# A decoder layer in split fp32: turned key buffers, a later latent, query splits moved into the first attention step, weight splits by GpSimd

## What is computed

```
x = x + memory_attention(layernorm(x))     # 8 heads used, sig = elu(q)+1, (sig @ M) / (sig @ z + eps), @ Wo.T
x = x + cross_attention(layernorm(x), ctx) # 16 sequences of 64 queries, 64 context and 64 latent keys,
                                           # 4 key heads x 8 query heads of 128, softmax, @ Wo
x = x + experts(layernorm(x))              # router: softmax over 64, top 8; out = flat * w_sum + w_dense @ expert_bias
```

## Time and profile before

| | |
|---|---|
| median of three runs | 720.72 us (719.70 to 722.87) |
| the profiled execution | 720.87 us |
| its span, first to last instruction | 719.1 us |
| mean granted clock of TensorE, of full speed | 0.993 |
| busy: PE, its weight loads, DVE, ACT, POOL | 96%, 81%, 71%, 49%, 16% |
| the chain that ended last, by engine | PE 83%, DVE 8%, DMA 2%, ACT 2%, POOL 1% |
| moved | 90.1 MB, 125 GB/s over the span |

### The profile page before, as it was taken

The page is one execution under the profiler, slowest core; times in us unless marked ns, Lnnn a source line. Parts: engine busy times, 40 slices in busy tenths (PEclk is TensorE's granted clock), DMA queues, the critical chain, the costliest instruction groups (busy, mean ns, idle before and its releaser), DMA issues.

```text
span 719.1 us, 10998 instructions
## 1 busy us (share of the span) xinstructions
PE 692.9 (96%) x3562; PEld 581.1 (81%) x3562; DVE 510.3 (71%) x1078; ACT 349.5 (49%) x1042; POOL 115.8 (16%) x121
## 2 busy tenths in 40 slices
PE   8999699999999998999999999999999999899995
PEld 6888588887887787888888888888888888688874
DVE  2764877678725878677677876767977566778876
ACT  4454655456244446344445643554645336555541
POOL 0175400000101332020120220210202000022410
PEclk9999999999999999999999999999999999999998
DMA  9888510001234456543242833423542404221101
GB/s 329 296 288 286 205 59 1 1 0 59 88 118 143 135 170 206 189 147 100 77 126 80 263 102 102 146 87 110 194 146 78 146 31 154 75 82 59 59 16 58
DMA packets 69997, 90.14 MB, mean 125 GB/s; under 512 B 4224, under 2 KB 47232, under 8 KB 69952
## 3 DMA queue, kind: packets, MB, share of 16 engines
q1 hardware_dynamic: 64160, 80.13, 34.2%
q10 hardware_dynamic: 5792, 9.44, 3.7%
HBM read 62.29 MB, written 27.26 MB: 125 GB/s over the span
## 4 chain that ended last, share of the span: by engine, by line
PE 83%; DVE 8%; DMA 2%; issue 2%; ACT 2%; POOL 1%; SPq 0%; POOLq 0%; ACTq 0%; DVEq 0%
PE bank L896 23%; PE bank L828 19%; PE bank L652 14%; PE bank L965 7%; PE bank L1014 5%; PE bank L798 5%; PE bank L991 4%; PE bank L643 1%; DMA raw<-in_L_attn_Wo 1%; PE bank L765 1%; DVE regA L1364 1%; PE bank L687 1%; PE bank L731 1%; DVE forms L1364 1%; DMA raw<-in_ctx 1%
## 5 line engine op out<-in xcount | busy, mean ns | idle before, releaser
L896 PE MATMUL bank<-regA,oT 128*128 128x512 f32 x768 | 180.6, 391 | 3.1 <-DVE oT L1364 3.1
L896 PEld LDWEIGHTS bank<-regA,oT 128*128 128x128 f32 x768 | 143.4, 188 | 33.3 <-DVE oT L1364 3.9
L1290 ACT ACTIVATE probs<-bank,negmax 128x128 f32<-128x128 f32 x256 | 90.1, 378 | 46.0 <-DVE negmax L1741 46.0
L828 PE MATMUL bank<-xnT,forms 128*128 128x512 f32 x384 | 97.2, 397 | 0.2
L828 PEld LDWEIGHTS bank<-xnT,forms 128*128 128x128 f32 x384 | 70.1, 188 | 15.2 <-DVE qbuf L1571 1.7
L828 PE MATMUL bank<-regC,forms 128*128 128x512 f32 x288 | 75.8, 401 | 2.4 <-DVE qbuf L1571 2.4
L1044 ACT CAST oT<-bank 128x512 fp32r<-128x512 f32 x64 | 37.6, 588 | 79.3 <-PE bank L1014 76.5
L1044 ACT CAST pT<-bank 128x512 fp32r<-128x512 f32 x64 | 34.7, 592 | 69.5 <-PE bank L991 69.5
L652 PE MATMUL bank<-regC,xnT 128*128 128x512 f32 x256 | 67.8, 396 | 0.0
L965 PEld LDWEIGHTS bank<-k_ring,qbuf 128*128 128x128 f32 x512 | 62.0, 191 | 2.5
L828 PEld LDWEIGHTS bank<-regC,forms 128*128 128x128 f32 x288 | 52.8, 190 | 12.9 <-DVE qbuf L1571 2.4
(11 more groups left out here) (151 smaller groups left out, 1072.0 us busy)
## 6 DMA issues: line engine op xcount, KB each, us to landing
q_dram<-qbuf SPq DMA_DIRECT2D x32, 512.0 KB, 3.0
qbuf<-q_dram SPq DMA_DIRECT2D x31, 512.0 KB, 4.5
raw<-in_L_attn_Wo SPq DMA_DIRECT2D x8, 1024.0 KB, 7.6
raw<-in_L_xattn_Wo SPq DMA_DIRECT2D x4, 2048.0 KB, 9.9
wq_raw<-in_L_xattn_Wq SPq DMA_DIRECT2D x16, 512.0 KB, 4.1
k_ring<-keys_dram SPq DMA_DIRECT2D x32, 128.0 KB, 3.6
v_raw<-vals_dram SPq DMA_DIRECT2D x64, 64.0 KB, 3.5
rawk<-in_L_xattn_Wv SPq DMA_DIRECT2D x4, 512.0 KB, 4.0
```

The lines of the kernel that those rows point to most:

```text
L828: last = nc.tensor.matmul(k_bank[:, :], forms[:, p[1], a, i, c, :], right(b)[:, c, :], start=j == 0, stop=j == 5)
L896: last = nc.tensor.matmul(bank[7][:, :], oT[:, a, h, :], wo[:, b, h, :], start=h == 0 and i == 0, stop=h == GH - 1 and i == 2)
L1290: last = nc.scalar.activation(probs[:, bb, p, :], bank[bb][:, p * P:(p + 1) * P], ACT.Exp, bias=negmax[:, bb, p:p + 1], accum_out=rowsum[: ...
```

## The change

- The three buffers of `save_kv` are used in the order `kvout`, `qb`, `qneg`. ACT waits ahead of its loop for buffer 2, DVE for buffer 1, and for buffer 0 only ahead of its first denominators.
- The sixth latent's transposes, cast and split move from loop turn 17 to turn 18 on PE, ACT and DVE.
- The second split of the key weights leaves turn 18: ACT's casts go behind the third value copy, DVE's splits behind the eighth latent.
- The three summed casts and splits of pair 5 leave the last turn of the lead loop for the first attention step, on ACT behind the value cast, on DVE behind the value split. SP's program is as before.
- In step 0 of every group but the first ACT's last four weight casts go ahead of its context casts (`oT`). In group 3 DVE splits heads 0 and 1 ahead of its context splits, 2 and 3 behind them, and POOL splits 4 to 7.
- In step 7 of group 2 and step 1 of group 3 the last two heads of the projection go behind the probability transposes (in step 1 of group 3 so behind the router transposes too).

```diff
-        kv_slots = (qneg[:, :], qb[:, :], kvout[:, :])
+        kv_slots = (kvout[:, :], qb[:, :], qneg[:, :])
...
             def scale_expert(e):
...
+            for h in range(4, GH):
+                pool.wait_ge(wo_hi, GH * (KV - 1) + h + 1)
+                pool.wait_ge(wo_lo, GH * (KV - 1) + h)
+                nc.gpsimd.tensor_tensor(wo[:, 1, h, :], wo_raw[:, h, :], wo[:, 0, h, :].bitcast(F), ALU.subtract)\
+                    .then_inc(wo_lo, 1)
...
-                if output_in(i):
+                if output_in(i) and i != 2 * NT + 1:
                     latent_transposes(output_in(i) - 1)
+                if i == 2 * NT + 2:
+                    latent_transposes(output_in(i - 1) - 1)
...
-            def project(g, t, release):
+            def project(g, t, release, heads=range(GH)):
...
-                pe.wait_ge(oT_lo, 2 * n + 2)
-                pe.wait_ge(proj_added, n + 1)
-                for h in range(GH):
+                if heads[0] == 0:
+                    pe.wait_ge(oT_lo, 2 * n + 2)
+                    pe.wait_ge(proj_added, n + 1)
+                for h in heads:
...
+                divided = not pair and not (last_group and t >= 2) and t
+                front = range(GH - 2) if divided else range(GH)
                 if not first_step:
                     if t == 0:
                         project(g - 1, 7, True)
                     else:
-                        project(g, t - 1, False)
+                        project(g, t - 1, False, front)
...
                 elif pair:
                     product_5(pair)
                     product_3(pair)
+                elif divided:
+                    project(g, t - 1, False, range(GH - 2, GH))
...
-            act.wait_ge(kv_written[0], kv_count(0, 16))
+            act.wait_ge(kv_written[2], kv_count(2, 16))
...
-                if i == 2 * NT + 2:
-                    wkv_high(1, wkv2, 2, 0)
-                if output_in(i):
-                    latent_high(output_in(i) - 1)
+                    latent_high(output_in(i - 1) - 1)
...
+                if t == 2:
+                    wkv_high(1, wkv2, 2, 0)
...
                 copy_1(p)
-                summed_high(p + 1, (p + 1) % 2)
+                if p < LEAD:
+                    summed_high(p + 1, (p + 1) % 2)
...
-                if t % 2 and has_pair(g, t + 2):
+                if first_step or t % 2 and has_pair(g, t + 2):
                     summed_high(pair + 1, slot)
...
+                if t == 0 and not first_step:
+                    act.wait_ge(proj_done, 8 * g)
+                    for h in range(4, GH):
+                        wo_high(g, h)
                 for bb in range(2):
...
-                if t == 0 and not first_step:
-                    act.wait_ge(proj_done, 8 * g)
-                    for h in range(4, GH):
-                        wo_high(g, h)
...
+                    if s == 0:
+                        dve.wait_ge(kv_written[0], kv_count(0, 16))
...
-            for r in (1, 2):
-                dve.wait_ge(kv_written[r], kv_count(r, 16))
+            dve.wait_ge(kv_written[1], kv_count(1, 16))
...
-                if i == 2 * NT + 2:
-                    wkv_low(1, wkv2, 3 * KC, 0)
...
             x_low(tr("latent", NT - 1), NT - 1)
+            wkv_low(1, wkv2, 3 * KC, 0)
...
-                summed_low(p + 1, (p + 1) % 2)
                 if p < LEAD:
+                    summed_low(p + 1, (p + 1) % 2)
...
-                if t % 2 and has_pair(g, t + 2):
+                if first_step or t % 2 and has_pair(g, t + 2):
                     summed_low(p + 1, slot)
...
-                    for h in range(2 if p is not None else 0, 4):
+                    for h in range(2) if p is None else range(2, 4):
                         wo_low(g, h)
...
-                    for h in range(4, GH):
+                    for h in range(2, 4) if p is None else range(4, GH):
                         wo_low(g, h)
```

More of the change, by code:

```diff
@@ L1211, in _ @@
                     wkv_high(0, wkv2, 2, 1, (2 * (i % 2), 2 * (i % 2) + 1))
+                if output_in(i) and i != 2 * NT + 1:
+                    latent_high(output_in(i) - 1)
                 if i == 2 * NT + 2:
-                    wkv_high(1, wkv2, 2, 0)
-                if output_in(i):
-                    latent_high(output_in(i) - 1)
+                    latent_high(output_in(i - 1) - 1)
             def save_latent_values(t):
@@ L1529, in _ @@
                     wkv_low(0, wkv2, 2 * KC, 1, (2 * (i % 2), 2 * (i % 2) + 1))
+                if output_in(i) and i != 2 * NT + 1:
+                    x_low(tr("latent", output_in(i) - 1), output_in(i) - 1)
                 if i == 2 * NT + 2:
-                    wkv_low(1, wkv2, 3 * KC, 0)
-                if output_in(i):
-                    x_low(tr("latent", output_in(i) - 1), output_in(i) - 1)
+                    x_low(tr("latent", output_in(i - 1) - 1), output_in(i - 1) - 1)
                 if output_in(i) is not None and i != 2 * NT - 1:
```

## The result

| | before | after |
|---|---|---|
| median | 720.39 us (6 runs, 719.70 to 724.12) | 733.02 us (6 runs, 729.97 to 734.99) |
| the profiled execution | 720.87 | 734.94 |
| its span | 719.1 | 733.1 |
| mean granted clock of TensorE | 0.993 | 0.982 |

The ratio of the times is 1.016, with a 95% interval from 1.0124 to 1.0195. The ratios in this document are not exactly quotients of two medians (that would be 1.0175 here); where two edits are compared, the ratios decide, because every group of runs was set against its own runs of the kernel before. The change makes the kernel slower, by 12.6 us of the medians, 11.5 by the ratio. The forecast was 731.4 us in a range from 723 to 736.

A forecast was written before the change was run, and what follows sets the result against it. The prediction took TensorE, busy 96% of the span, as the bound. Its terms, 0 - 0.6 + 2.6 + 1.3 - 1.0 + 4.85 + 3.4 = +10.55, added to 720.87 gave 731.4 us, range 723 to 736.

The forecast's parts named there:

- Part 1: Memory stage, key buffers turned: `sig` could start earlier, gain given back at POOL's folds; 0, ends -5.6 and +1.7 us.
- the race of 72.30 against 72.33: Memory stage: `sig` would start at 72.30, POOL's fold at 72.33; just ahead or just behind, gain taken as 0.
- Part 2: Latent values, sixth latent's transposes later: PE then waits for the seventh, with one DVE split less ahead; -0.6 us.
- Part 3: Latent values, second key weight split later: block sums +5.05 us, PE pauses before the second latent key product; +2.6 us.
- Part 4: First attention step, splits behind first maxima: the second step's query load comes late, PE pauses 4.65 us; net +1.3 us.
- Part 5: Late output weights: -1.0 us in step 7 of group 2, +4.85 us from step 0 of group 3.
- (a): Step 7 of group 2: two heads, 1.37 us of PE, fill the pause of 1.01 before 602.82; -1.0 us.
- (b): Group 3, from step 0: POOL's four splits delay SP's router load, PE pauses 5.9 us before router transposes; +4.85 us.
- The clock: TensorE's granted clock falls once behind each of the pauses of 4.65 and 5.9 us; together +3.4 us.
- the clock stays up: Rival: TensorE's clock stays at its upper level behind both long pauses; 728.0 us, chance 0.18.
- The port went DVE's way: Rival, memory stage: DVE gets the shared port ahead of POOL and both PE pauses vanish; 725.8 us, chance 0.10.
- the loads are in time: Rival: second step's query slice and the router rows land before PE needs them; 717.2 us, chance 0.12.

The follow-up runs named there:

- a1: The changed kernel with the second key weight split put into slots where ACT and DVE idle; 727.13 us, ratio 1.009.
- a2: The changed kernel with SP loading pair 6 behind the first attention step's key, query and value loads instead of ahead; 726.93 us, ratio 1.0079.
- b5: The kernel before with the key buffers turned and POOL's last fold held until the second `sig` is done; 719.41 us, ratio 0.9985.
- b1: The kernel before with the key buffers turned and nothing else; 721.30 us, ratio 1.0013.
- a5: The changed kernel with 40 throwaway identity transposes on PE at the end of its first attention step; 730.93 us, ratio 1.0136.
- b6: The kernel before, key buffers as they were, with POOL's last fold held until the second `sig` is done; 718.73 us, ratio 0.9992.

## Why the prediction held, and where it was off

*Part 1, at 0.* The number was right, by luck in part. Of the two ways that the prediction gave for the race of 72.30 against 72.33, the kernel after shows one, `sig` ahead by 0.06: the denominators go through one by one between POOL's operations and the second pause grows. The kernel with the buffers alone shows the other. But the second pause did not grow by what the first lost: the first lost 2.2 us and the second grew by 0.4. What made 0 of the remaining 1.8 us is a fall of the clock behind the second pause, at 3.22, which stood only in the upper end of the part. The other traces agree. With the buffers turned and the folds free, the two pauses together are 2.2 to 4.4 us in nine traces (5.6 and 4.6 in the two with the buffers as before), but the granted clock fell behind the last of them in seven of the nine (0.62 to 0.65 over 4.5 us) and in neither of the two. That the buffers bring the fall is not shown by so few. The Trainium skill (SBUF — State Buffer, Who interferes with whom) states that a DVE instruction with two SBUF inputs contends with a GpSimd instruction that reads SBUF, and that the order of issue decides who blocks. The trace agrees: the 0.28 product that met an operation of POOL took 1.38, and `sig` 2.40 against 0.69 when it was first.

*Part 2, at -0.6.* PE's waits for the sixth and seventh latent were 1.13 and 0.41 us and are nothing and 1.13, so -0.4. The -0.5 of the table has part 1 in it, and a start of the stage 0.3 later (DVE's first biased query at 70.53 for 70.26).

*Part 3, at +2.6.* The pause was 2.62, through the five engines' steps as they were named. Its fall of the clock (0.66, 1.5 to 1.6 us) was left at the end of the range.

*Part 4, at +1.3.* The pause was 4.62 for 4.65, the landing 5.7; +1.6 at the second scores.

*Part 5.* (a) -1.3 for -1.0. (b) The pause was 5.33 for 5.9, POOL's four operations 6.08 for 6.4 (from 618.45 to 624.9). Two took 1.30 and two 1.55, beside DVE's probabilities, with 0.13 between: the disturbance was about 0.25 each and not 0.5. The 0.5 was said to come from the overlaps in rows 3, but those show DVE held by POOL and not the reverse. From issue to PE's transposes it was 4.9 for 5.1. +4.6 for 4.85.

*The clock* is where the sum was off. Two falls at 1.7 were counted, 3.4 us; the traced execution has four, and they took 1.7, 1.6, 2.7 and 2.6, together 8.6. The price was read from a window of 0.62 behind a short pause, a mixture of the levels. Behind the two long pauses PE got 0.50 throughout. That is 5.2 us more than in the sum, less 1.8 for part 1's shorter pauses; with small errors of both signs elsewhere the traced span grew by 14.0 where 10.55 were forecast. The median, 733.0, lies 1.6 above 731.4. The queues and their prices were right, but that the total came so near has luck in it: the traced execution is 3.5 us above the forecast, and 1.8 us of error in part 1's pauses hid as much of the clock's.

*The rivals.* That the clock stays up did not come true behind the long pauses: 0.50 behind both here, and 0.50 again in the runs that kept one of them (behind 4.06 in the run with the router later, behind 5.35 and 5.42 in the runs of a1 and a2). The port went DVE's way in the kernel after at the first `sig`, and the waits did not vanish. That the loads are in time was priced at -3.3 for the first step and 717.2 us in all. It didn't come true, but as a price it was good: the run with the loads moved gained 3.0 in that step, and 717.2 less the 2.6 of part 3, which that price still held, is 714.6, where the version in which all three are in time took 713.94.

Not tried: how the fall of the clock could be avoided behind the memory stage's pause, and whether a longer chain of POOL's splits could run before ACT's casts.

## What to carry to other kernels

Moving work off the path an engine waits on is paid at the next queue. Before a step is put later, list what every engine and the transfer queue hold in program order behind its last signal: two of the three losses here were loads that stood behind a split which had become later. One load was moved ahead, the consumer of the other was moved by a step, and the splits of the third loss went into idle slots; that turned 1.6% slower into 0.8% faster. Price a new pause with the low clock that may follow it: here another 1.5 to 2.7 us where it came.

## What the runs showed of the hardware

- Between 1.9 and 2.9 us the length of a pause did not decide whether the clock falls. Granted clock over 4.5 us behind PE's pauses in these traces: 0.62 behind 1.97 (before, first attention step), 0.66 behind 1.88 (b5), 0.65 behind 2.26 (the mended version), 0.62 behind 2.68 (b1), 0.66 behind 2.62 (after, latent values), 0.50 behind the same 2.62 in the run with the filler (a5); but 1.00 behind 2.77 and 2.86, behind 1.99 (b6), behind 2.48 (mended, buffers as before), behind 2.78 (a2), and behind the very pause of 2.62 before the latent key product in the run with the router later, whose program is the same up to there. Behind each of the eight pauses of 4.06 us and more it fell: to 0.50, but for a1's 4.46 with 0.66. What else decides is open.
- A start 0.06 us ahead or 0.12 us behind a fold changed the length of the same `sig` from 0.69 to 2.79 us, and made the first pause 2.68 instead of 0.59 and the second nothing instead of 3.22.
- Both effects differ between executions of kernels with the same program in that stage, so a stage's gain of 1 to 2 us has to be read in several traces.
